# An output stage paced by tiles instead of groups of four, with mean-free rows and one-hots made by VectorE

## What is computed

```
x = x + recurrence(layernorm(x), ctx, ctx, ...)          # x1, written to memory by the kernel's first stage
h = layernorm(x)                                         # the experts' input
probs = softmax(h @ Wg); idx = sorted top_k(probs, cap)  # 16 experts, each takes 2 of the 32 rows at each position
q, k, v per expert; att = q k^T; p = softmax over positions
ao = (p @ v) @ Wo + bo                                   # per expert and chosen row, 512 features
y = h; y[chosen rows] += ao                              # scatter-add
out = x + (y - mean(y)) * rsqrt(var(y) + 1e-5) * ln_g + ln_b
```

## Time and profile before

| | |
|---|---|
| median of three runs | 1844.03 us (1843.45 to 1845.11) |
| the profiled execution's own time | 1843.14 us |
| its span (first to last instruction in the trace) | 1841.3 us |
| output stage, first A to the end of the last F | 1446.0 to 1834.9 us |
| busy share of the span: PE, DVE, ACT, POOL | 85%, 77%, 66%, 69% |

### The profile page before, as it was taken

The page is one execution under the profiler, slowest core; times in us unless marked ns, Lnnn a source line. Parts: engine busy times, 40 slices in busy tenths (PEclk is TensorE's granted clock), DMA queues, the critical chain, the costliest instruction groups (busy, mean ns, idle before and its releaser), DMA issues. The chain is left out here.

```text
span 1841.3 us, 58322 instructions
## 1 busy us (share of the span) xinstructions
PE 1571.0 (85%) x21933; PEld 1273.1 (69%) x22061; DVE 1414.6 (77%) x3007; ACT 1210.4 (66%) x2950; POOL 1266.8 (69%) x1235
## 2 busy tenths in 40 slices
PE   4899999999999999999999996899997877777763
PEld 3777777777777777777777775799996544444431
DVE  2578788787787787787787777687755399999998
ACT  3677777777777777777777764233332887878873
POOL 1576776777777767767777776578872568687664
PEclk9999999999999999999999998899998998989987
DMA  6123222232222322323223111745653176767776
GB/s 214 54 88 105 88 97 97 88 105 88 96 97 88 104 89 90 103 88 101 92 88 106 48 37 64 272 133 158 198 148 78 28 183 146 190 167 181 187 184 160
DMA packets 82021, 217.72 MB, mean 118 GB/s; under 512 B 13136, under 2 KB 14544, under 8 KB 72784
## 3 DMA queue, kind: packets, MB, share of 16 engines
q1 hardware_dynamic: 71504, 180.42, 33.3%
q0 software_dynamic: 10240, 33.56, 6.1%
HBM read 146.82 MB, written 67.11 MB: 116 GB/s over the span
## 5 line engine op out<-in xcount | busy, mean ns | idle before, releaser
L316 POOL TENSOR_TENSOR rec_hn<-rec_hn,rec_out_w 128x512 f32<-128x512 f32 x128 | 199.7, 1560 | 180.1 <-DVE rec_hn L743 180.1
L294 POOL TENSOR_TENSOR rec_hrs<-rec_harg,rec_minus_half 128x8 f32<-128x8 f32 x128 | 253.8, 1983 | 10.0
L1316 POOL TENSOR_TENSOR out_x_half<-out_x_half,ln_b 128x512 f32<-128x512 f32 x128 | 170.9, 1365 | 98.0 <-DVE out_z_half L1496 96.8
L1435 PE MATMUL out_z_ps<-probs_all,out_hot 128*128 128x512 f32 x256 | 150.3, 671 | 98.5 <-ACT probs_all L1362 52.4
L540 ACT ACTIVATE rec_d<-rec_l_ps 128x512 f32<-128x512 f32 x256 | 150.4, 587 | 41.0 <-PE rec_l_ps L448 40.7
L1004 PE MATMUL exp_q_ps<-exp_wqkv,exp_rows_t 128*128 128x192 f32 x1024 | 177.2, 327 | 0.0
L709 DVE TENSOR_TENSOR rec_c<-rec_s_ps,rec_d 128x512 f32<-128x512 f32 x256 | 164.5, 684 | 14.6 <-PE rec_s_ps L424 14.6
L1060 ACT ACTIVATE exp_rows_t<-exp_t_ps 128x512 f32<-128x512 f32 x128 | 69.4, 594 | 151.3 <-PE exp_t_ps L992 120.1
L955 POOL DMA_INDIRECT exp_x_rows<-x_scratch,rowid x128 | 135.5, 1059 | 45.3 <-issue 25.9
L763 DVE TENSOR_TENSOR rec_x_ring<-rec_x_ring,rec_hn 128x512 f32<-128x512 f32 x128 | 88.6, 692 | 100.3 <-POOL rec_hn L316 99.9
L1004 PEld LDWEIGHTS exp_q_ps<-exp_wqkv,exp_rows_t 128*128 128x128 f32 x1024 | 165.4, 190 | 0.4 <-ACT exp_rows_t L1060 0.3
(11 more groups left out here) (210 smaller groups left out, 4494.7 us busy)
## 6 DMA issues: line engine op xcount, KB each, us to landing
rec_x_ring<-in_x SPq DMA_DIRECT2D x128, 256.0 KB, 2.7
rec_ctx_ring<-in_ctx SPq DMA_DIRECT2D x128, 256.0 KB, 2.9
x_scratch<-rec_x_ring SPq DMA_DIRECT2D x128, 256.0 KB, 2.0
out_x_half<-x_scratch SPq DMA_DIRECT2D x128, 256.0 KB, 5.1
out<-out_x_half SPq DMA_DIRECT2D x128, 256.0 KB, 4.0
exp_wqkv<-in_wqkv SPq DMA_DIRECT2D x4, 1536.0 KB, 7.4
exp_x_rows<-x_scratch,rowid POOLq DMA_INDIRECT x128
wo<-in_wo SPq DMA_DIRECT2D x1, 2048.0 KB
```

Source lines behind the costliest of these rows:

```text
L294: nc.gpsimd.tensor_tensor(hrs[:, G % 2], harg[:, G % 2], mhalf[:], ALU.pow).then_inc(hrs_done, 1)
L316: nc.gpsimd.tensor_tensor(h, h, w8[:], ALU.mult).then_inc(hw_done, 1)
L1316: nc.gpsimd.tensor_tensor(xt[H % XR][:, q, :], xt[H % XR][:, q, :], lb[:], ALU.add).then_inc(xb_done, 1)
L1435: nc.tensor.matmul(z_ps[T % 3][:], hot[T % 4][:], ao[T % 4], start=True, stop=True).then_inc(z_full, 1)
```

## The change

It does four things.

1. The mean of z is made zero ahead of time, so that it need not be computed. Each column of the output weights and the bias loses its mean over features (`wo_centred`, on ScalarE in the expert stage at m = 40 to 55, and `bo_mean` on VectorE), and the mean of each x1 row, which the first stage now keeps (`moments`), is brought into tile order by a fourth `by_row` (16 more small matmuls) as `centres`. A subtracts it. All squares are then summed on ScalarE (L1391 of the changed kernel), and the two tiny instructions, bn_stats and bn_aggr and the accumulator outputs of A are gone.
2. The one-hots of four tiles are made by one VectorE comparison of 128x512 (`mark`, L1482 of the changed kernel). ScalarE's two instructions for each tile are gone.
3. VectorE works tile by tile: in iteration T it does A(T), S(T-3), F(T-7), and after each fourth iteration a mark. GpSimd's loop goes by tiles too, with the power at the second tile of a half and attend at the third.
4. There are eight z buffers of one tile and five x1 buffers of a half; the fifth lies in the part of `v_all` that has been used up. A load is issued five halves ahead, right after the store of the half that held its buffer, and so has to wait for that store to land.

```diff
-    XR, ZR, LEAD, ON_ACT = 4, 2, 18, 3
+    XR, ZR, LEAD, SCALE, FINISH = 5, 8, 18, 3, 7
...
     @block.sync
...
-        for H in range(3):
+        for H in range(XR):
             load(H)
         for H in range(HALVES):
             sp.wait_ge(out_done, 4 * (H + 1))
             for j in range(4):
                 sp.dma_start(o_view[H, j], xt[H % XR][j * NB:(j + 1) * NB]).then_inc(o_st[H % XR], 16)
-            if H + 3 < HALVES:
-                load(H + 3)
+            if H + XR < HALVES:
+                load(H + XR)
...
     @block.gpsimd
...
+        for T in range(TILES + 3):
+            if T < TILES:
+                pool.wait_ge(z_read, T + 1)
+                x1 = xt[T // 4 % XR][:, T % 4, :]
+                nc.gpsimd.tensor_tensor(x1, x1, lb[:], ALU.add).then_inc(xb_done, 1)
+            H, q = divmod(T, 4)
+            if q == 1 and H:
+                pool.wait_ge(square_done, 4 * H)
+                nc.gpsimd.tensor_tensor(ve[H % 2][:], var[H % 3][:], epsv[:, 4 * H - 4:4 * H], ALU.add).then_inc(ve_done, 1)
+                pool.wait_ge(ve_done, H)
...
+                nc.gpsimd.tensor_tensor(rs[H % 3][:], ve[H % 2][:], mhalf[:], ALU.pow).then_inc(rs_done, 1)
+            if q == 2 and T < TILES:
...
+                    attend(c + 1, n)
...
     @block.vector
...
+        def mark(H):
+            full = [P, 4, P]
+            if H >= 2:
+                dve.wait_ge(z_full, 4 * (H - 1))
+            vec.tensor_tensor(hot[H % 2][:], tokid[:].unsqueeze(1).broadcast_to(full),
+                              colv[:, 4 * H:4 * H + 4].unsqueeze(2).broadcast_to(full), ALU.is_equal).then_inc(hot_done, 1)
+
+        def add(T):
+            H, q = divmod(T, 4)
+            if q == 0:
+                dve.wait_ge(x_in[H % XR], 64 * (H // XR + 1))
+            if T >= ZR:
+                dve.wait_ge(out_done, T - ZR + 1)
+            dve.wait_ge(z_full, T + 1)
+            vec.scalar_tensor_tensor(zt[T % ZR][:], xt[H % XR][:, q, :], centres[:, T:T + 1], z_ps[T % 3][:],
+                                     ALU.subtract, ALU.add).then_inc(z_read, 1)
+
+        def scale(T):
+            dve.wait_ge(square_done, T + 1)
+            vec.tensor_tensor(zt[T % ZR][:], zt[T % ZR][:], lg[:], ALU.mult).then_inc(zg_done, 1)
+
+        def finish(T):
+            H, q = divmod(T, 4)
+            x1 = xt[H % XR][:, q, :]
             dve.wait_ge(rs_done, H + 1)
+            dve.wait_ge(xb_done, T + 1)
+            dve.wait_ge(zg_done, T + 1)
+            vec.scalar_tensor_tensor(x1, zt[T % ZR][:], rs[(H + 1) % 3][:, q:q + 1], x1, ALU.mult, ALU.add
+                                     ).then_inc(out_done, 1)
...
+        for T in range(TILES + FINISH):
+            if T < TILES:
+                add(T)
+            if 0 <= T - SCALE < TILES:
+                scale(T - SCALE)
+            if T >= FINISH:
+                finish(T - FINISH)
+            if T % 4 == 3 and T // 4 + 2 < HALVES:
+                mark(T // 4 + 2)
```

More of the change, by code:

```diff
@@ L1029, in _ @@
                 pe.wait_ge(mean_read, NE)
[L1030 to L1032 removed]
+                by_row(0, lambda c: idx[:, c].rearrange("p h i -> p (h i)"))
+                by_row(1, lambda c: ssel[:, c].rearrange("p h i -> p (h i)"))
+                by_row(2, lambda c: var[:, c])
+                by_row(3, lambda c: moments[:, :, c, 0]).then_inc(tables_full, 1)
+            if m == 52:
+                pe.wait_ge(out_in, 64)
+                nc.tensor.matmul(m_ps[1][:, 0:KC], mean[:], bo[:], start=True, stop=True).then_inc(bo_full, 1)
             if m > 0:
@@ L1312, in _ @@
             attend(1, n)
[L1313 to L1328, removed]
+        for T in range(TILES + 3):
[8 more added lines that the diff above has]
+                pool.wait_ge(ve_done, H)
+                if H > 3:
+                    pool.wait_ge(out_done, 4 * (H - 3))
+                nc.gpsimd.tensor_tensor(rs[H % 3][:], ve[H % 2][:], mhalf[:], ALU.pow).then_inc(rs_done, 1)
+            if q == 2 and T < TILES:
+                c, n = divmod(H + 3, 8)
+                if H == 0:
+                    attend(1, 2)
+                if n < 4 and c + 1 < NC:
+                    attend(c + 1, n)
     def projected(u):
@@ L1362, in put_rows, with square @@
             nc.scalar.activation(ao[T % 4], r_ps[T % 2][:], ACT.Copy, scale=sgs[:, T:T + 1]).then_inc(r_read, 1)
[L1364 to L1375, removed]
-                if H or q:
-                    act.wait_ge(square_done, ON_ACT * H + q)
-                nc.scalar.activation(dump[:], zt[H % ZR][:, q, :], ACT.Square, bias=offs[H % 2][:, q:q + 1],
-                                     scale=-E ** -0.5, accum_out=agg[H % 2][:, q, 1:2]).then_inc(square_done, 1)
+        def square(T):
+            H, q = divmod(T, 4)
+            act.wait_ge(z_read, T + 1)
+            act.wait_ge(square_done, T)
+            if H >= 3:
+                act.wait_ge(ve_done, H - 2)
+            nc.scalar.activation(dump[:], zt[T % ZR][:], ACT.Square, scale=E ** -0.5,
+                                 accum_out=var[(H + 1) % 3][:, q:q + 1]).then_inc(square_done, 1)
         for n in range(4):
             put_sums(n)
-        for T in range(-LEAD, TILES):
-            if T > 0 and T % 4 == 0:
-                deviations(T // 4 - 1)
+        for T in range(-LEAD, TILES + 1):
             if T % 2 == 0 and T + LEAD < 2 * PIECES:
```

122 lines of the change are left out of this document (47 added, 75 removed).

## The result

The changed kernel takes **1878.36 us** (median of 4 runs, 1877.29 to 1879.58), beside 1844.57 for the kernel before on the same chip: ratio 1.0182, 95% interval 1.0165 to 1.020. It is slower, as forecast, and 6.4 us above the 1872 of the prediction, inside its range. The profiled execution took 1877.29 us.

What follows compares the result with a forecast made beforehand. VectorE was taken to set the output stage's pace. Terms +36.8, +7.2, +2.5, -5.4, -1.4, -13 and +0.9 made +27.6 us, which counted from the median 1844.03 gave 1872 us; range 1838 to 1890.

Steps and rivals of the forecast that it cites:

- The mechanism: Output stage: GpSimd's P (x1 + ln_b) runs between S and F, and F waits 1.02 us for each, 4.08 a half.
- Rival 1: Output stage: P hides under an A and costs 0.35 us; 1805 us, with 16% for 1800 to 1838.
- Rival 4: Output stage: TensorE's clock may fall to 1.2 GHz, so TensorE sets the pace; 1890 to 1920 us, 5%.
- the signs of being wrong that I named: Changed kernel's profile: F stays near 0.74, A is held up, or VectorE waits for z_ps or for the power.
- the power: GpSimd's L1323, before the third tile's P: may push that P under an A; bounds 0 and 26 us, middle -13 taken.
- halves 0 and 1: Start of the output stage, 29.4 us: ScalarE loses eight marks and gains two sums of squares, -5.4 us.
- 21 halves without attend: Output stage, halves 2 to 30 without attend: 12.99 us each against 11.24 before, +36.8 us.
- eight halves with attend: Output stage, halves with an attend on GpSimd: 14.2 us each against 13.3 before, +7.2 us.
- last half, and the one ahead of it: End of the output stage: the last half, from its first A, takes 19.1 us against 16.6, +2.5 us.
- lead-in and expert stage: Before the output stage: two ScalarE marks gone, -1.4 us; 16 more matmuls and the bias's mean, +0.9 us.
- stores at the end: Stores behind the last half: claimed to stay as they were, with no time added.
- The half without P: VectorE's A, S, F, mark and waits in one output-stage half, before P's cost is added: 8.91 us.

Runs made afterwards that it cites:

- P behind F: The changed kernel with one wait more: GpSimd's P (x1 + ln_b) of a tile also waits for F(T-7); 1843.66 us.
- the order by halves: The changed kernel with VectorE's loop put back to four A, four S, four F of the half before, and a mark; 1835.62 us.
- the run with a sum written: The changed kernel with F as a tensor_scalar that reads z alone and also writes its sum to an unread column; 1791.37 us.

## Why the prediction was right

**The mechanism** held: P runs between S and F, all four P of a half are exposed, F waits 1.02 us for each. Shown by taking P away, by taking its reads away, by changing F's form, and by moving P. Rival 1 asked for P under an A; it didn't get there by itself (F takes 0.74 us only seven times, all after the last P), but "P behind F" and the order by halves put it there in part, and both are faster than the changed kernel. Rival 4, TensorE's clock, is out: it was granted 0.98 in the even stretch, close to full 2.4 GHz, and its scatter waits for VectorE. Of the signs of being wrong that I named, one showed: F waited for the power, once and for 3.7 us, inside the halves 0 and 1 that were sized right.

**The sum**, in us of span; 1841.3 + 34.2 = 1875.5:

| term | forecast | measured |
|---|---|---|
| 21 halves without attend | +36.8 (12.99 each) | +31.3 (12.73) |
| the power | -13 | 0 |
| eight halves with attend | +7.2 (14.2) | +5.2 (13.98), and +0.8 in the half behind |
| halves 0 and 1 | -5.4 | -5.3 (24.1 for 29.4) |
| last half, and the one ahead of it | +2.5 | +2.0 (18.6), and -0.4 |
| lead-in and expert stage | -0.5 | -0.6 |
| stores at the end | 0 | +1.4 |
| all | +27.6 | +34.4 worked out, 34.2 by the spans |

- *The half without P* (forecast 8.91, is 8.66 to 8.70): A, S, F and the mark were sized within 0.01 each. The wait for the F right in front costs 0.12, not 0.18: F to A is 1.80 here, and F to the mark, which doesn't wait, 1.68. In the earlier trace rows another 0.06 was in the gap that I read as the wait. What I left out of the price of before is the 0.6 us that P took there from the tiny tensor_scalar (777 ns in the mean, and 184 without P). It didn't enter the sum, since that started from the measured 11.24.
- *The power* is the step that failed: "the rows don't decide between them, so I take the middle". They are not two ends of a range but two outcomes, and the middle was neither. The power took 1.02 us (median 1018 ns), the P behind it came 0.17 us ahead of F, and F waited as always. My count of that tile for 1.02 us, "about 0.2 us before F", was right; the text should have said 1885 or 1859 and given each a chance. With 0 for this term the sum gives 1885, and the smaller half (-5.5) and the attends bring it to within 1 us of what was measured. That 1872 was only 6.4 us off is in part luck: 13 us taken off for nothing stood against some 7 us that the other terms had too much.
- *Attends* fell mostly under A and its wait, as said.
- *Stores*: "The stores behind it stay" was wrong by 1.4 us. The last seven F follow each other without any A, so the last two halves finish 2.65 us apart (1865.05 to 1867.7) and eight issues stand in SP's queue (6.84 us) where four stood.

## What to carry to other kernels

Before an order is changed on VectorE, list which of its instructions GpSimd's reads hold up and which they don't (here A, with one operand in PSUM, never over 0.749 us, and bn_stats, never over 0.685), and see under which of them each GpSimd instruction will be asked for; the interleaving that looks smoothest can put every one of them in front of an F. Count such a collision for each GpSimd instruction (here 1.02 us for a P of 1.27), and against it weigh the instructions saved: here 42 us saved and 77 lost. Where a term has two outcomes depending on a few tenths of a microsecond, give both their times and chances instead of the mean.

## What the runs showed of the hardware

- A quicker instruction can be the worse one: tensor_scalar of 128x512 in 0.47 us is held up by GpSimd's reads (1.49), the same with an accumulated sum in 0.73 is not. The tiny tensor_scalar of 128x3 took 777 ns in the mean in the kernel before and 184 without P.
- A GpSimd tensor_tensor of 128x512 that takes 1.27 us alone held F up for 1.02, as scalar_tensor_tensor of two operands from SBUF and as tensor_scalar of one; a memset of the same size (0.53 us) held neither S nor F up.
- A wait of A for the F right in front cost 0.12 us from start to start (1.80 for 1.68), and with three instructions between nothing.
- The power of 128x4 took 1.02 us in the changed kernel and mostly 1.34 to 1.40 in others (before, by halves, P behind F), and 1.56 in the run with a sum written. What sets this was not tested.
